# Two chunks of W side by side for each block of h in a LoRA feed-forward, with adapter passes grouped by block and PSUM waits by bank

## The chip, the cores and the metric

The kernel runs on one NeuronCore of one Trainium2 chip. The metric is the device time of one execution in microseconds (us); lower is better. TensorE, VectorE (DVE), ScalarE (ACT), GpSimd (POOL) and SyncE (SP) each follow their own list of instructions and meet at semaphores.

## The reference

Per batch of 8, with 512 rows (four tiles of 128) and 2048 columns:

```python
x = x + autocorrelation(layernorm(x), ctx, ctx)      # first block: spectra, top 12 lags, rolled sums
x = x + ffn(layernorm(x))                            # second block

def ffn(h):                                          # h: [8, 512, 2048], W: [2048, 2048]
    base = h @ W + bias
    A = einsum('bn,nri->bri', gate, lora_A)          # the batch's adapter, rank 32
    B = einsum('bn,nor->bor', gate, lora_B)
    return base + (h @ A.T) @ B.T + (h @ A_shared.T) @ B_shared.T
```

The change lies in the second block alone.

## The kernel before

Two blocks follow each other. The first computes the autocorrelation and stores `x2` in DRAM; it also splits W in two fp16 parts, `w_hi` and `w_lo`, and stores them. The second block loads all of W into SBUF (four chunks of 512 output columns, 16 blocks of 128 rows each) and runs over 32 tiles, `b` for the batch (0 to 7) and `t` for the tile in it (0 to 3), n = 4b + t. Batch 0 and batch 7 are written out, the others are a loop on some engines.

**h.** A tile of `x2` is loaded to one of two buffers `xt`. POOL adds the last row of `ctx` (`add_last`, L1292), DVE takes mean and variance (`statistics`, ends at `nb2`, L1472), ACT makes `h` (`normalise`, L1322) and its fp16 part, DVE the rest (`rest_of_h`, L1478), each in two halves, and ACT's queue issues four DMA transposes into `h_hi` and `h_lo` (L1334, L1336). POOL then adds the bias into `xt` (L1300). `h` of tile n+1 is made while TensorE works on tile n.

**TensorE.** A product in near fp32 is three fp16 passes: high by high, high by rest, rest by high. `chunk` (L1400) makes one bank of PSUM (0 to 3) from 16 blocks, 48 passes of 512 columns (L1412 to L1414). Each pass names its stationary block (here a block of `h`) and has a weight load of its own. In the middle of chunk 0 the small product `ax` is transposed (L1419). `adapter_out` (L1422) multiplies it with the adapters: for each of the four banks 4 to 7 one pass over 128 rows of `axT` (L1432) and one over 64 rows (L1433). `step` (L1435) is chunk 0, `adapter_out`, chunks 1, 2, 3, then `adapter_in` of the next tile (L1378), 48 passes of 64 columns that need all four transposes of the next `h`. `chunk` waits for `y_ok` to reach 4n: all four banks of the tile before have been read.

**DVE** (`step`, L1563) goes in a fixed order: rest of `ax`; `statistics` of the next tile; `finish` 0 (L1519: bank 0 into `xt`, waits for `y_spec` of that chunk, raises `y_ok`); `add_adapter` (banks 4 to 7, L1508); at t=3 the scales and the rest of the next batch's adapters; `finish` 1; `rest_of_h`; three sums of the next batch's adapter (`gated_sum`, L1532, each with a load `sg` from DRAM into one of two buffers; load i waits for sum i-2); `finish` 2; up to three more sums; at t=2 `largest` (L1541); `finish` 3; `adapter` of the next tile (`ax`, L1485). At t=2 only one sum stands between `finish` 2 and `largest`. Batch 7 has no sums.

**SP** goes in a fixed order too: the loads of `sg` for the tile; at t=2, once the last sum is done, the store of `b_next` (L1233) and, when that has landed, two loads of `b_f` (L1214); then it waits for `y_ok` 4n+4, stores `xt` to `out` (L1268), waits for that to land, loads `xt` for tile n+2 (L1210), and at t=2 the next `vl` (L1238).

```python
sp.wait_ge(y_ok, 4 * n + 4)
sp.dma_start(out_t[b, :, t, :], xt[:, t % 2, :]).then_inc(s_out[t % 2], 16)
...
finish(b, t, 2)
if gated and t < TT - 1:
    gated_part(b, t, 1)
...
finish(b, t, 3)
```

Of the kernel before, what the change touches and what calls it, by code (L numbers as in the profile page):

```python
# [41 lines left out]
KT = D // P  # L42
NL, RANK = 16, 32
# [38 lines left out]
def ahead(b, g, k):  # L82

    c = (g + k) // GPB
    return (b + c if c else b), (g + k) % GPB
# [7 lines left out]
def later(b, i):  # L93

    return not (isinstance(b, int) and b == 0 and i == 0)


def build(nc, x, ctx, gate, w, bias, lora_ab, lora_as, lora_bsT, fwd_tab, inv_tab, eye, nyq_mask, fwd_pair, out):
# [9 lines left out]
    with ExitStack() as outer:  # L108
        def sb(name, shape, dt=FP32, where=outer):
            return where.enter_context(nc.sbuf_tensor(name, shape, dt))  # L110

        def sem(name, where=outer):
            return where.enter_context(nc.semaphore(name))
# [19 lines left out]
        ps = outer.enter_context(nc.psum_tensor("ps", [P, 8, 512], FP32))  # L133
# [15 lines left out]
        s_w = [sem(f"s_w{k}") for k in range(8)]  # L149
# [1000 lines left out]
        with ExitStack() as st:  # L1150
            b_f = sb("b_f", [4 * RANK, D], FP32, st)
            b_hi = sb("b_hi", [4 * RANK, D], FP16, st)
            sb("early", [P, 79872 // 4], FP32, st)
            b_lo = early["b_lo"]
            h_hi = [early["h_hi0"], sb("h_hi1", [P, KT, P], FP16, st)]
            h_lo = [early["h_lo0"], sb("h_lo1", [P, KT, P], FP16, st)]
            w_hi, w_lo = [early["w_hi0"]], [early["w_lo0"]]
# [13 lines left out]
            axT = sb("axT", [4 * RANK, P], FP16, st)  # L1171
# [27 lines left out]
            d_spec = sem("d_spec", st)  # L1199
            d_ok = sem("d_ok", st)  # L1200
            y_spec = sem("y_spec", st)
            y_ok = sem("y_ok", st)

            with nc.Block() as block:
# [171 lines left out]
                @block.tensor  # L1376
                def _(pe):
                    def adapter_in(b, t):  # L1378

                        n, k = TT * b + t, t % 2  # L1380
                        pe.wait_ge(s_hh, 32 * n + 32)
                        for q in range(2):
                            pe.wait_ge(s_hl[q], 16 * n + 16)
                        if later(b, t):
                            pe.wait_ge(d_ok, 4 * n)
                        if t == 0:
                            pe.wait_ge(ab_lo, 16 * b + 8)
                        dst = ps[:, 4, 0:2 * RANK]
                        for i in range(KT):
                            high, rest = (a[:, i, :, :].rearrange("p s r -> p (s r)") for a in (a_hi, a_lo))  # L1390
                            nc.tensor.matmul(dst, h_hi[k][:, i, :], high, start=(i == 0), stop=False)  # L1391
                            nc.tensor.matmul(dst, h_hi[k][:, i, :], rest, start=False, stop=False)  # L1392
                            last = nc.tensor.matmul(dst, h_lo[k][:, i, :], high, start=False, stop=(i == KT - 1))  # L1393
                        last.then_inc(ax_spec, 1)

                    def bounds(b, bank, col):
                        pe.wait_ge(mx_ok, b + 1)
                        nc.tensor.matmul(ps[:, bank, col:col + 4], ones[:, :], mx[:, :], start=True, stop=True).then_inc(sc_spec, 1)

                    def chunk(b, t, c, gated):  # L1400
                        n, k = TT * b + t, t % 2
                        if c == 0:
                            pe.wait_ge(s_hh, 32 * n + 32)
                            for q in range(2):
                                pe.wait_ge(s_hl[q], 16 * n + 16)
                        if later(b, t):
                            pe.wait_ge(y_ok, 4 * n)
                        cols = slice(c * 512, (c + 1) * 512)
                        for i in range(KT):
                            if not later(b, t) and i % (KT // 2) == 0:  # L1410
                                pe.wait_ge(s_w[2 * c + i // (KT // 2)], 32)
                            nc.tensor.matmul(ps[:, c, :], h_hi[k][:, i, :], w_hi[c][:, i, :], start=(i == 0), stop=False)  # L1412
                            nc.tensor.matmul(ps[:, c, :], h_hi[k][:, i, :], w_lo[c][:, i, :], start=False, stop=False)  # L1413
                            last = nc.tensor.matmul(ps[:, c, :], h_lo[k][:, i, :], w_hi[c][:, i, :], start=False, stop=(i == KT - 1))  # L1414
                            if c == 0 and i == KT // 2:
                                pe.wait_ge(ax_ok, n + 1)
                                if gated and t == TT - 1:
                                    bounds(b + 1, 5, 2 * P)
                                nc.tensor.transpose(ps[:, 5, 0:P], ax[:, :, :].rearrange("p s r -> p (s r)"), ident[:, :]).then_inc(axt_spec, 1)  # L1419
                        last.then_inc(y_spec, 1)  # L1420

                    def adapter_out(b, t, gated):  # L1422

                        n = TT * b + t
                        pe.wait_ge(axt_lo, n + 1)
                        if gated and t == TT - 1:
                            pe.wait_ge(sc_read, b + 2)
                        if t == 0:
                            pe.wait_ge(ab_lo, 16 * b + 16)
                        for c in range(4):  # L1430
                            cols = slice(c * 512, (c + 1) * 512)
                            nc.tensor.matmul(ps[:, 4 + c, :], axT[:, :], b_hi[:, cols], start=True, stop=False)  # L1432
                            nc.tensor.matmul(ps[:, 4 + c, :], axT[0:2 * RANK, :], b_lo[0:2 * RANK, cols], start=False, stop=True).then_inc(d_spec, 1)  # L1433

                    def step(b, t, more, gated):  # L1435
                        chunk(b, t, 0, gated)
                        adapter_out(b, t, gated)
                        chunk(b, t, 1, gated)
                        chunk(b, t, 2, gated)
                        chunk(b, t, 3, gated)  # L1440
                        if more:
                            adapter_in(*ahead(b, t, 1))

                    bounds(0, 5, 2 * P)
                    adapter_in(0, 0)
                    for t in range(TT):
                        step(0, t, True, True)
                    for b in range(1, B - 1):
                        for t in range(TT):
                            step(b, t, True, True)  # L1450
                    for t in range(TT):
                        step(B - 1, t, t + 1 < TT, False)
# [190 lines left out]
```

## Time and profile before

| | |
|---|---|
| time, median of 3 runs | 3146.86 us (3145.36 to 3148.0) |
| the profiled execution | 3147.78 us, span 3146.0 us |
| TensorE busy | 3044.8 us (97%) |
| VectorE, ScalarE, GpSimd busy | 2080.5, 1117.0, 1675.4 us |
| mean granted TensorE clock | 0.988 |
| second block | about 1659 us to the end |
| passes of the four chunks (L1412 to L1414) | 3 x 2048, on the chain that ended last for 3 x 14% of the span |

A pass's busy time (379 ns) includes its way through the array and overlaps the next; how fast passes go is read from the distance between their starts. A clock of 1.00 is 2.4 GHz, 0.50 is 1.2 GHz. "idle before" names what ended the idle time of an engine.

### The profile page before, as it was taken

What the parts mean: (1) busy time and instruction counts of PE and PEld (TensorE: products, weight loads), DVE (VectorE), ACT (ScalarE), POOL (GpSimd) and SP (SyncE); (2) the same over time, 40 slices, a digit from 0 to 9 for tenths busy, and PEclk for the clock granted to TensorE, in tenths of its full rate; (3) what the DMA queues carried; (4) which work ended last, traced back from release to release, by engine and by line L of the source; (5) the groups of instructions that cost most, each with busy time, mean ns of one, the idle gap of its engine ahead of it and who ended that gap; (6) DMA issues with size and microseconds to landing.
All of it is one profiled execution on the core that took longest, in us unless ns stands there. A gap on an engine that the chain in (4) does not pass through costs nothing. (4 is left out here: it accounts for less than half of the span.)

```text
span 3146.0 us, 37959 instructions
## 1 busy us (share of the span) xinstructions
PE 3044.8 (97%) x14387; PEld 1642.7 (52%) x14387; DVE 2080.5 (66%) x2741; ACT 1117.0 (36%) x1696; POOL 1675.4 (53%) x753
## 2 busy tenths in 40 slices
PE   5999999999989999999977999999999999999999
PEld 3656566565656566566533444444444444444444
DVE  6899999999989999899984434443444444344321
ACT  4666666666656666555421110110111011011100
POOL 4888898888979898898651221221122112112210
PEclk8999999999999999999988999999999999999999
DMA  6334434344354534434259434344343534444321
GB/s 233 126 125 148 148 137 167 122 150 151 133 170 134 181 137 141 161 108 150 81 184 281 141 106 150 100 128 150 108 134 108 158 91 138 141 122 123 94 74 40
DMA packets 280787, 430.26 MB, mean 137 GB/s; under 512 B 147440, under 2 KB 163952, under 8 KB 265072
## 3 DMA queue, kind: packets, MB, share of 16 engines
q1 hardware_dynamic: 145456, 394.43, 36.0%
q10 hardware_dynamic: 135168, 33.57, 6.0%
q8 instruction: 113, 1.85, 0.2%
q14 instruction: 50, 0.41, 0.0%
HBM read 308.15 MB, written 86.25 MB: 125 GB/s over the span
## 5 line engine op out<-in xcount | busy, mean ns | idle before, releaser
L1412 PE MATMUL ps<-w_hi,h_hi 128*128 128x512 f16 x2048 | 776.8, 379 | 1.0 <-DVE xt L1519 1.0
L1413 PE MATMUL ps<-w_lo,h_hi 128*128 128x512 f16 x2048 | 776.4, 379 | 0.0
L1414 PE MATMUL ps<-w_hi,h_lo 128*128 128x512 f16 x2048 | 776.4, 379 | 0.0
L1292 POOL TENSOR_TENSOR xt<-xt,vl 128x2048 f32<-128x2048 f32 x31 | 139.6, 4503 | 919.4 <-DMA xt<-x_scratch 678.4
L877 PE MATMUL ps<-op,it 128*128 128x512 f32 x1024 | 447.3, 595 | 12.8 <-DVE op L1023 12.8
L802 PE MATMUL ps<-wt,fp 128*128 128x512 f16 x1536 | 338.3, 380 | 1.4 <-DVE wt L990 1.4
L1414 PEld LDWEIGHTS ps<-w_hi,h_lo 128*128 128x128 f16 x2048 | 200.4, 98 | 241.9 <-issue 0.4
L1412 PEld LDWEIGHTS ps<-w_hi,h_hi 128*128 128x128 f16 x2048 | 200.6, 98 | 240.9 <-issue 8.7
L877 PEld LDWEIGHTS ps<-op,it 128*128 128x128 f32 x1024 | 195.1, 191 | 247.3 <-issue 230.5
L1413 PEld LDWEIGHTS ps<-w_lo,h_hi 128*128 128x128 f16 x2048 | 200.5, 98 | 230.8 <-issue 0.3
L802 PEld LDWEIGHTS ps<-wt,fp 128*128 128x128 f16 x1536 | 150.5, 98 | 184.1 <-issue 1.9
L867 PE MATMUL ps<-it,cp 128*128 128x256 f32 x1024 | 230.7, 384 | 15.4 <-ACT cp L612 15.4
L1343 ACT ACTIVATE axT<-ps 128x128 f16<-128x128 f32 x32 | 8.9, 277 | 666.7 <-PE ps L1419 666.7
L1519 DVE SCALAR_TENSOR_TENSOR xt<-ps,w_back,xt 128x512 f32<-128x512 f32 x128 | 95.8, 748 | 209.0 <-PE ps L1414 198.6
L1461 DVE BATCH_NORM_STATS2 bn<-xt 128x6 f32<-128x512 f32 x124 | 76.6, 681 | 232.7 <-POOL xt L1292 232.7
L867 PEld LDWEIGHTS ps<-it,cp 128*128 128x128 f32 x1024 | 197.4, 193 | 46.7 <-ACT cp L612 16.4
L1532 DVE SCALAR_TENSOR_TENSOR ab<-sg,gt,ab 128x1024 f32<-128x1024 f32 x105 | 134.7, 1283 | 105.3 <-DMA sg<-lora_ab 104.4
L1322 ACT ACTIVATE h<-xt,nb,rs 128x2048 f32<-128x2048 f32 x31 | 64.9, 2095 | 371.5 <-DVE nb L1472 371.5
L1300 POOL TENSOR_TENSOR xt<-xt,brow 128x2048 f32<-128x2048 f32 x32 | 144.7, 4523 | 86.3 <-ACT h L1322 80.8
L452 POOL TENSOR_TENSOR cgl<-cg,uh 128x1024 fp32r<-128x1024 f32 x64 | 177.5, 2794 | 20.5 <-ACT uh L606 20.5
L475 POOL TENSOR_TENSOR cp<-eo 128x1024 f32<-128x1024 f32 x31 | 85.8, 2769 | 184.8 <-DVE cr L928 184.8
L794 PE MATMUL ps<-uh,fth 128*128 128x512 f32 x384 | 156.4, 407 | 17.2 <-POOL cgl L452 17.2
(190 smaller groups left out, 5724.2 us busy)
## 6 DMA issues: line engine op xcount, KB each, us to landing
sg<-lora_ab SPq DMA_DIRECT2D x112, 512.0 KB, 4.5
xv<-x SPq DMA_DIRECT2D x33, 1024.0 KB, 5.2
cg<-ctx SPq DMA_DIRECT2D x32, 1024.0 KB, 5.2
x_scratch<-xv SPq DMA_DIRECT2D x32, 1024.0 KB, 6.6
xt<-x_scratch SPq DMA_DIRECT2D x32, 1024.0 KB, 5.0
out<-xt SPq DMA_DIRECT2D x32, 1024.0 KB, 3.9
xg<-x SPq DMA_DIRECT2D x30, 1024.0 KB, 8.4
xrow<-x SPq DMA_DIRECT2D x24, 1024.0 KB, 6.0
```

The lines of the kernel that those rows point to most:

```text
L452: nc.gpsimd.tensor_tensor(cgl[:, k, 2 * h:2 * h + 2, :], cg[:, k, 2 * h:2 * h + 2, :], uh[:, 2 * h:2 * h + 2, :], ALU.subtract).then_inc(u ...
L794: last = nc.tensor.matmul(ps[:, TURN[kind], :], tab, val, start=(fresh and r == 0 and i == 0), stop=(r == 1 and i == 2), skip_group_check= ...
L802: last = nc.tensor.matmul(ps[:, bank, :], fp[:, tab, k, kind, :], pair[val][:, 2 * part + k, :], start=(k == 0 and i == 0), stop=(k == 1 a ...
L867: last = nc.tensor.matmul(ps[:, TURN[j], h * HALF:(h + 1) * HALF], cp[:, s, j * P:(j + 1) * P], it[:, s, :], start=(i == 0), stop=(i == 1))
L877: last = nc.tensor.matmul(ps[:, 4 + TURN[t], :], it[:, s, (t % 2) * P:(t % 2 + 1) * P], op[:, t // 2, s, :], start=(s == 0), stop=(s == 3))
L1292: nc.gpsimd.tensor_tensor(xt[:, k, :], xt[:, k, :], vl[:, :], ALU.add).then_inc(vl_ok, 1)
L1300: nc.gpsimd.tensor_tensor(xt[:, t % 2, :], xt[:, t % 2, :], brow[:, :], ALU.add).then_inc(bias_ok, 1)
L1412: nc.tensor.matmul(ps[:, c, :], h_hi[k][:, i, :], w_hi[c][:, i, :], start=(i == 0), stop=False)
L1413: nc.tensor.matmul(ps[:, c, :], h_hi[k][:, i, :], w_lo[c][:, i, :], start=False, stop=False)
L1414: last = nc.tensor.matmul(ps[:, c, :], h_lo[k][:, i, :], w_hi[c][:, i, :], start=False, stop=(i == KT - 1))
L1519: nc.vector.scalar_tensor_tensor(out=xt[:, k, cols], in0=ps[:, c, :], scalar=w_back[:, 0:1], in1=xt[:, k, cols], op0=ALU.mult, op1=ALU.add ...
L1532: nc.vector.scalar_tensor_tensor(out=ab[:, 0::2, :], in0=sg[:, i % 2, :, :], scalar=gt[:, i:i + 1], in1=ab[:, 0::2, :], op0=ALU.mult, op1= ...
```

## The change

Three edits, all in TensorE's list.

1. `chunk_pair` takes two chunks at once. For each block i it makes the four passes with `h_hi` (two chunks by `w_hi` and `w_lo`) and then the two with `h_lo`. The pair's last two passes raise `y_spec`, one after the other. The transpose of `ax` comes after block 8 of the first pair, `adapter_out` after the first pair.
2. `adapter_out` makes the four passes over 128 rows first and then the four over 64 rows.
3. The first pair waits for `y_ok` 4n-2 and the second for 4n.

DVE, SP, ACT and POOL keep their lists.

```diff
-                    def chunk(b, t, c, gated):
+                    def chunk_pair(b, t, first, gated):
                         n, k = TT * b + t, t % 2
-                        if c == 0:
+                        pair = (first, first + 1)
+                        if first == 0:
                             pe.wait_ge(s_hh, 32 * n + 32)
                             for q in range(2):
                                 pe.wait_ge(s_hl[q], 16 * n + 16)
                         if later(b, t):
-                            pe.wait_ge(y_ok, 4 * n)
-                        cols = slice(c * 512, (c + 1) * 512)
+                            pe.wait_ge(y_ok, 4 * n - 2 + first)
                         for i in range(KT):
                             if not later(b, t) and i % (KT // 2) == 0:
-                                pe.wait_ge(s_w[2 * c + i // (KT // 2)], 32)
-                            nc.tensor.matmul(ps[:, c, :], h_hi[k][:, i, :], w_hi[c][:, i, :], start=(i == 0), stop=False)
-                            nc.tensor.matmul(ps[:, c, :], h_hi[k][:, i, :], w_lo[c][:, i, :], start=False, stop=False)
-                            last = nc.tensor.matmul(ps[:, c, :], h_lo[k][:, i, :], w_hi[c][:, i, :], start=False, stop=(i == KT - 1))
-                            if c == 0 and i == KT // 2:
+                                for c in pair:
+                                    pe.wait_ge(s_w[2 * c + i // (KT // 2)], 32)
+                            for c in pair:
+                                nc.tensor.matmul(ps[:, c, :], h_hi[k][:, i, :], w_hi[c][:, i, :], start=(i == 0), stop=False)
+                                nc.tensor.matmul(ps[:, c, :], h_hi[k][:, i, :], w_lo[c][:, i, :], start=False, stop=False)
+                            for c in pair:
+                                last = nc.tensor.matmul(ps[:, c, :], h_lo[k][:, i, :], w_hi[c][:, i, :], start=False, stop=(i == KT - 1))
+                                if i == KT - 1:
+                                    last.then_inc(y_spec, 1)
+                            if first == 0 and i == KT // 2:
...
-                        last.then_inc(y_spec, 1)
...
                         for c in range(4):
-                            cols = slice(c * 512, (c + 1) * 512)
-                            nc.tensor.matmul(ps[:, 4 + c, :], axT[:, :], b_hi[:, cols], start=True, stop=False)
-                            nc.tensor.matmul(ps[:, 4 + c, :], axT[0:2 * RANK, :], b_lo[0:2 * RANK, cols], start=False, stop=True).then_inc(d_spec, 1)
+                            nc.tensor.matmul(ps[:, 4 + c, :], axT[:, :], b_hi[:, c * 512:(c + 1) * 512], start=True, stop=False)
+                        for c in range(4):
+                            nc.tensor.matmul(ps[:, 4 + c, :], axT[0:2 * RANK, :], b_lo[0:2 * RANK, c * 512:(c + 1) * 512],
+                                             start=False, stop=True).then_inc(d_spec, 1)
...
-                        chunk(b, t, 0, gated)
+                        chunk_pair(b, t, 0, gated)
                         adapter_out(b, t, gated)
-                        chunk(b, t, 1, gated)
-                        chunk(b, t, 2, gated)
-                        chunk(b, t, 3, gated)
+                        chunk_pair(b, t, 2, gated)
```

## Rows read from the trace of the kernel before

**Rows 1.** Windows: busy us and count by engine, granted clock, DMA share, GB/s.

```profile
2600.00:2800.00 200.00, 200.00 (x1079) 91.86 (x1077) 82.96 (x121) 24.31 (x21) 45.89 (x15) 1.00 0.42 126
```

**Rows 2.** Groups by form, passes and weight loads: busy us, mean ns | idle before.

```profile
L1412 PE MATMUL ps<-w_hi,h_hi 128*128 128x512 f16 x2048 | 776.8, 379 | 1.0 <-DVE xt L1519 1.0
...
L1413 PEld LDWEIGHTS ps<-w_lo,h_hi 128*128 128x128 f16 x2048 | 200.5, 98 | 230.8 <-issue 0.3
```

**Rows 3.** Timeline of PE, batch 1, t=2: `adapter_out`'s first pass, first passes of chunks 1 and 2.

```profile
1966.71 0.38 PE L1432 MATMUL ps<-b_hi,axT 128*128 128x512 f16 x1
...
1969.27 0.39 PE L1412 MATMUL ps<-w_hi,h_hi 128*128 128x512 f16 x1
...
1979.64 0.38 PE L1412 MATMUL ps<-w_hi,h_hi 128*128 128x512 f16 x1
```

**Rows 4.** Timeline of weight loads, end of an `adapter_out` and start of a chunk.

```profile
2013.35 0.09 PEld L1433 LDWEIGHTS ps<-b_lo,axT 64*128 64x128 f16 x1 [0.23 <-issue]
2013.67 0.10 PEld L1432 LDWEIGHTS ps<-b_hi,axT 128*128 128x128 f16 x1 [0.23 <-issue]
...
2014.97 0.10 PEld L1413 LDWEIGHTS ps<-w_lo,h_hi 128*128 128x128 f16 x1
```

**Rows 5.** Timeline of DVE, batch 5: `finish` 2 and 3 of t=2, `nb2` in t=3.

```profile
2722.20 0.75 DVE L1519 SCALAR_TENSOR_TENSOR xt<-ps,w_back,xt 128x512 f32<-128x512 f32 x1
...
2730.92 0.75 DVE L1519 SCALAR_TENSOR_TENSOR xt<-ps,w_back,xt 128x512 f32<-128x512 f32 x1 [5.49 <-PE ps L1414]
...
2751.74 0.21 DVE L1472 TENSOR_SCALAR nb<-mv,rs 128x1 f32<-128x1 f32 x1
```

**Rows 6.** Timeline of SP's queue, batch 5, t=2.

```profile
2724.20 0.33 SPq L1233 DMA_DIRECT2D b_next_scratch<-ab  x1
2726.27 0.80 SPq L1214 DMA_DIRECT2D b_f<-b_next_scratch  x2
2731.84 0.36 SPq L1268 DMA_DIRECT2D out<-xt  x1
```

**Rows 7.** Timeline of PE, batch 5: first pass of `adapter_in` behind t=2 and behind t=3.

```profile
2730.72 0.19 PE L1391 MATMUL ps<-a_hi,h_hi 128*128 128x64 f16 x1
...
2776.40 0.19 PE L1391 MATMUL ps<-a_hi,h_hi 128*128 128x64 f16 x1
```

**Rows 8.** Timeline of ACT's queue: last transposes issued in t=2 and t=3 of batch 5.

```profile
2715.78 1.36 ACTq L1336 DMA_TRANSPOSE h_lo<-h  x1
...
2770.45 1.36 ACTq L1336 DMA_TRANSPOSE h_lo<-h  x1
```

**Rows 9.** The line L1336: time from issue to landing of its transposes.

```profile
DMA to landing us min/median/max: 3.0/3.2/6.6
```

**Rows 10.** Timeline, batch 2, t=1: `nb2`, `finish` 2 and the store of `xt`.

```profile
2111.69 0.21 DVE L1472 TENSOR_SCALAR nb<-mv,rs 128x1 f32<-128x1 f32 x1
...
2130.16 0.74 DVE L1519 SCALAR_TENSOR_TENSOR xt<-ps,w_back,xt 128x512 f32<-128x512 f32 x1
...
2138.28 0.35 SPq L1268 DMA_DIRECT2D out<-xt  x1
```

**Rows 11.** Timeline of POOL, batch 5, t=3: `add_last`.

```profile
2743.39 4.50 POOL L1292 TENSOR_TENSOR xt<-xt,vl 128x2048 f32<-128x2048 f32 x1 [32.63 <-DMA vl<-ctx]
```

**Rows 12.** Timeline, batch 3: store of `xt` and next `add_last`, at t=1 and t=2.

```profile
2321.74 0.35 SPq L1268 DMA_DIRECT2D out<-xt  x1
...
2332.99 4.50 POOL L1292 TENSOR_TENSOR xt<-xt,vl 128x2048 f32<-128x2048 f32 x1 [31.11 <-DMA xt<-x_scratch]
...
2366.94 0.36 SPq L1268 DMA_DIRECT2D out<-xt  x1
...
2380.39 4.51 POOL L1292 TENSOR_TENSOR xt<-xt,vl 128x2048 f32<-128x2048 f32 x1 [32.06 <-DMA vl<-ctx]
```

**Rows 13.** Windows at the end of the first block, a long idle of PE and after.

```profile
1636.00:1641.00 5.00, 0.00 (x0) 0.00 (x0) 4.96 (x6) 0.00 (x0) 4.92 (x4) 0.50 0.66 214
1641.00:1643.00 2.00, 1.92 (x3) 0.89 (x4) 0.03 (x1) 0.03 (x1) 2.00 (x2) 0.50 0.47 184
```

## The prediction

> **What bounds the kernel now.** I read the windows first. In the second block (from 1659 us to the end) TensorE is busy without a gap at the full granted clock, 1.00, which is 2.4 GHz [rows 1]. The groups by form say the same: before the first passes of a block of `h` TensorE idled 1.0 us in the whole stage, and each of its weight loads has a record of its own, 98 ns against a pass that issues every 0.216 us [rows 2, 3]. So in this stage time is issued passes times their spacing, plus any new wait. Everything else (DVE's epilogue, the adapter sums, the chain that makes the next `h`) is hidden, and the question is how deep.
>
> Where passes are not 0.216 us apart, the timeline shows it. From one block of W to the next are 48 passes in 10.37 us, 0.216 each; the 8 passes of `adapter_out` take 2.56 us, 0.320 each [rows 3]. The loads tell why: between two passes over 128 rows the load starts with the pass ahead of it and costs nothing (L1413 at 2014.97, no idle), while between a 128-row pass and a 64-row one, either way, the load port idles 0.23 us first and the load then lies bare [rows 4].
>
> **Part 1, `adapter_out` by stationary block.** Before: high, low, high, low ..., eight changes of shape for a tile (the one into `chunk` 1 included). After: four high, four low, two changes. Six times 0.104 us is 0.62 us per tile, and 32 tiles give 20.0 us. The trace has no 64-row pass behind a 64-row pass. Bounds: if its load hides, like every load between passes of one shape, 20.0; if 64 rows themselves are the trouble, only the three high-after-high places gain, 0.31 per tile, 10.0 us. I take 20.0, since 128-row loads pay 0.104 as well when the shape changes.
>
> Beside this stands a rule of the Trainium skill ("TensorE: Matmul & The Clock Gate", Part 3, the mechanism): a load overlaps passes in flight only when its row group differs. By it no pass behind one of the same rows would gain, and this edit would be worth nothing. The trace disagrees for 128 rows, where 2048 loads of L1413 idle behind nothing [rows 2, 4]; for 64 rows no run here shows it, and my lower bound is that case.
>
> **Part 2, pairs of chunks.** No pass is dropped: 96 per pair, the same six per `i`. Four passes now share a stationary block, but each still issues its load: before, L1413 already repeats the block of L1412 and has 2048 loads [rows 2]. They were hidden, so this gives 0. Banks now alternate every two passes; `adapter_out` changes bank every two passes at no cost beyond the change of shape, so 0 too. The transpose moves from 5.8 to 11.7 us into a tile, and `ax` is there by then (below, +8).
>
> **Part 3, the waits by bank.** The first pair waits for two epilogues of the tile before instead of four: this takes away the 1.0 us [rows 2]. I count -1.0.
>
> **Part 4, what moves on DVE.** `y_spec` for chunk 2 no longer comes 10.4 us before chunk 3's, but one pass before it. DVE's order is fixed: `finish` 2, up to three adapter sums, `finish` 3. So in tiles 0 to 2 of a batch the second half of the sums, done under chunk 3 until now, stands between the end of the passes and `finish` 3. Behind `finish` 3 queue, on SP, the store of `xt` and the load of the tile after next; behind that load POOL's `add_last`, DVE's statistics, `normalise`, the transposes of `h`, and at last `adapter_in`, which waits for all four of them.
>
> The tightest place is the last tile of a batch (t=3), where ACT and DVE make the adapters too. I take batch 5. Let a be the start of `adapter_in` behind the passes of t=2 (2730.72). `finish` 3 starts at a+0.20, SP issues the store at a+1.12 [rows 5 to 7]. After the change `finish` 2 starts at a+0.20-0.22 = a-0.02. From its start to SP's `b_next` store are 2.00 us (finish and one sum), 2.07 until that has landed, 0.85 for the two loads of `b_f`: the store of `xt` is issued 4.92 later, at a+4.90, and `finish` 3, behind `largest`, is done by then [rows 5, 6]. The chain starts 3.78 us later. Before, it had this slack: last transpose issued 2770.45, landed 3.2 later at 2773.65, `adapter_in` at 2776.40, so 2.75 us [rows 7 to 9]. The deadline comes 0.62 earlier by part 1. Stall: 3.78 + 0.62 - 2.75 = **1.65 us**, in 7 batches (the last makes no adapters): 11.6 us.
>
> In t=0 and t=1, `finish` 2 to the store takes 8.1 us [rows 10] against 1.1: 7.0 later. The `h` made in the tile after each has more slack, read in t=2: a transpose issued at 2715.78 and landed at latest 6.6 on, against 2730.72, is 8.3 us, and 7.6 are needed [rows 7 to 9]. No stall in t=1 and t=2, but 0.7 us from one. `ax`, read behind `finish` 3, comes at about +8 in the next tile, before the transpose at 11.7.
>
> Not all batches are like 5. In batch 3, store to `add_last` is 13.45 us against 11.55 [rows 6, 11, 12]: +1.9. And in t=0 and 1 the loop closes on itself: `nb2` to the store 26.4, store to `add_last` 11.25, `add_last` to `nb2` 8.56 [rows 5, 10 to 12], 46.2 against a tile of 44.9, so DVE is late by itself and the store of t=2 is 2.3 later still. Batch 3: 1.65+1.9+2.3 = 5.9. The same working gives extras of 2.8, 1.3, 1.0 and 1.4 for batches 2, 1, 4 and 6, and -0.2 for batch 0. Extras together 10.5; stalls 22.1 us.
>
> Do such stalls cost clock? In an idle of the first block that fills a window of 5 us the clock was at 0.50 (1.2 GHz), and right behind it three passes filled 2 us [rows 13]. The stalls here are 1.5 to 4.6 in one piece; I count nothing, and 2 us a batch where it happens.
>
> **Small ends.** At the very end `finish` 2 and 3 follow each other: 0.75-0.22, +0.5. At the start, chunk 3 of W, the last to be loaded, is needed one chunk (10.4 us) earlier. It is needed in the first tile alone; I count 0 and keep 2 us for the range.
>
> **Sum.** -20.0 - 1.0 + 22.1 + 0.5 = +1.6 us on the profiled execution's 3147.78 (span 3146.0 and 1.8 around it), which lies 0.9 above the median: 3148.5, say **3149 us**. The gain in issue is given back in seven waits.
>
> **Rivals.** A change under 0.2% (6.3 us) can't be told from none here.
>
> *Faster: the chain fits.* One mechanism, the slack ahead of `adapter_in` in t=3. Each us less on the chain is 7 us. With batch 5's stall everywhere, 11.6 us in all: 3138. With none: 3146.9-20-1+0.5 = 3126.4. It decides once the mean stall is under 2.0 us instead of 3.2. For it: the long way from store to `add_last` (13.45 us, not 11.55) is that of the middle batches, and may not come back. Against: the slack is read at both ends, and SP's order is fixed. Chance 0.32.
>
> *Slower: 64-row loads stay bare.* Part 1 gives 10.0, the deadline is 0.31 kinder and the stalls fall by 2.2: +9.5, 3156. Against: the equal price of both directions [rows 4]. This is also what the skill's rule on row groups would leave. Chance 0.12.
>
> *Slower: the chain is later than computed.* Sums waiting longer for loads of `sg` that now collide with the store and the transposes, t=2 stalling too, or the clock falling in the long stalls: 1 to 2 us a batch, 3156 to 3163. For it: t=0 and t=1 have 0.7 us left. Chance 0.17.
>
> *Bank changes cost clock.* A rule of the Trainium skill (same page, "A second HAM failure mode") has passes that cycle through PSUM banks let the clock swing between its levels. Here, `adapter_out` cycles through four banks and the clock is 1.00 over 200 us [rows 1, 3]. If a tenth of the 6144 passes ran at half clock it would be +133 us, 3280. Chance 0.02.
>
> *The pairing doesn't save loads* is in the forecast. If loads were dropped after all, the time is the same, since they are hidden.
>
> **Numbers.** Forecast 0.37 (3141 to 3154 as its own range), faster 0.32, bare loads 0.12, late chain 0.17, clock 0.02. Faster by over 0.2%: 0.31; within: 0.38; slower: 0.31. The range goes from half of the faster case's stalls to the late chain: 3131 to 3163.
>
> **What would show it.** `adapter_out` in 1.94 us with six passes 0.216 apart (right) or 2.25 (bare). As many loads as passes. `finish` 3 of t=0 and 1 some 8 us behind the passes. The first `adapter_in` pass of t=3 waiting for a transpose of `h_lo`, seven times, 1.5 to 4.6 us, none in the last batch. Wrong would be: waits in t=1 or t=2 as well, a store of `xt` at t=2 earlier than 3.8 us behind its old place, or a clock under 1.00 there.

## The result, and the profile after

The changed kernel takes 3168.4 us (median of 4; 3166.0 to 3171.6) against 3147.4 for the one before: ratio 1.0066, 95% interval [1.0054, 1.0078], 21 us slower. The forecast was 3149 with a range up to 3163. What it named as the cost is there, in its place and seven times, but about twice as dear.

First what was to be gained. The timeline of the changed kernel around an `adapter_out` (start, duration; "x4" is four passes in a row):

```profile
2674.34 0.74 PEld L1435 LDWEIGHTS ps<-b_hi,axT 128*128 128x128 f16 x4
2674.56 1.03 PE L1435 MATMUL ps<-b_hi,axT 128*128 128x512 f16 x4
2675.51 0.54 PEld L1437 LDWEIGHTS ps<-b_lo,axT 64*128 64x128 f16 x4 [0.42 <-issue]
2675.52 1.03 PE L1437 MATMUL ps<-b_lo,axT 64*128 64x512 f16 x4
2676.48 0.10 PEld L1414 LDWEIGHTS ps<-w_hi,h_hi 128*128 128x128 f16 x1 [0.42 <-issue]
2676.48 0.39 PE L1414 MATMUL ps<-w_hi,h_hi 128*128 128x512 f16 x1
```

The eight passes take 1.92 us instead of 2.56 [rows 3]. Only the two loads at a change of shape come late (the 0.42 us of idle); those between 64-row passes are hidden like the others. 0.64 us a tile, 20 us in all, as forecast. A tile without a wait is now 44.88 us from start to start, and 45.51 before.

The waits of the second block (us in total, times, longest us) and the groups, passes only (busy us, mean ns | idle before):

```profile
PE ps L1391 <- issue: 28.3, 7, 4.8
```

```profile
L1414 PE MATMUL ps<-w_hi,h_hi 128*128 128x512 f16 x2048 | 780.2, 381 | 0.0
...
L1391 PE MATMUL ps<-a_hi,h_hi 128*128 128x64 f16 x512 | 56.6, 204 | 32.2 <-issue 28.3 <-DVE a_lo L1499 3.9
L1437 PE MATMUL ps<-b_lo,axT 64*128 64x512 f16 x128 | 33.1, 379 | 0.0
...
L1435 PE MATMUL ps<-b_hi,axT 128*128 128x512 f16 x128 | 32.9, 379 | 0.0
```

The 1.0 us in front of the first pass of a block is gone [rows 2]. In its place stand seven waits ahead of `adapter_in`, 28.3 us by the view (it counts from the modelled end of the last pass, 0.17 us later than the next pass could start). "issue" names no releaser; the chain of batch 5, from t=2 into t=3, shows what it is. The same rows of before are [rows 5 to 9, 11]:

```profile
2742.08 0.75 DVE L1522 SCALAR_TENSOR_TENSOR xt<-ps,w_back,xt 128x512 f32<-128x512 f32 x1 [1.48 <-PE ps L1417]
2742.10 0.19 PE L1391 MATMUL ps<-a_hi,h_hi 128*128 128x64 f16 x1
...
2742.75 1.28 DVE L1535 SCALAR_TENSOR_TENSOR ab<-sg,gt,ab 128x1024 f32<-128x1024 f32 x1
2744.05 0.33 SPq L1233 DMA_DIRECT2D b_next_scratch<-ab  x1
2744.06 1.22 DVE L1544 TENSOR_REDUCE mx<-ab 128x2 f32<-128x1024 f32 x1
2745.20 0.74 DVE L1522 SCALAR_TENSOR_TENSOR xt<-ps,w_back,xt 128x512 f32<-128x512 f32 x1
...
2746.12 0.80 SPq L1214 DMA_DIRECT2D b_f<-b_next_scratch  x2
2747.21 0.36 SPq L1268 DMA_DIRECT2D out<-xt  x1
2752.79 0.37 SPq L1210 DMA_DIRECT2D xt<-x_scratch  x1
...
2761.14 4.51 POOL L1292 TENSOR_TENSOR xt<-xt,vl 128x2048 f32<-128x2048 f32 x1 [31.73 <-DMA vl<-ctx]
...
2769.50 0.21 DVE L1475 TENSOR_SCALAR nb<-mv,rs 128x1 f32<-128x1 f32 x1
...
2788.21 1.36 ACTq L1336 DMA_TRANSPOSE h_lo<-h  x1
...
2791.64 0.21 PE L1391 MATMUL ps<-a_hi,h_hi 128*128 128x64 f16 x1 [4.32 <-issue]
```

With a = 2742.10: `finish` 2 starts at a-0.02, the store of `b_next` is issued at a+1.95, the loads of `b_f` at a+4.02, the store of `xt` at a+5.11 (before: a+1.12). Then `add_last` 13.93 us later (before 11.55), `nb2` 8.36, the last transpose 18.71, `adapter_in` 3.43. The steps to `nb2` and to the last transpose are those of before, and the transpose lands after 3.2 us as before; the first pass follows 0.2 us later. TensorE was ready at a+45.05 and starts at a+49.54: 4.5 us late. The distances from last pass to `adapter_in`, less one pass, are 3.9, 3.7, 3.9, 4.0, 4.9, 4.5 and 4.6 us in batches 0 to 6: 29.5 us.

And this is not all. Windows from TensorE's last pass of that tile on (the last columns are the granted clock, the DMA share and GB/s):

```profile
2787.00:2791.00 4.00, 0.32 (x2) 0.00 (x0) 2.47 (x3) 0.00 (x0) 0.00 (x0) 0.98 0.78 166
2791.00:2796.00 5.00, 4.36 (x53) 3.29 (x54) 0.29 (x1) 0.00 (x0) 0.00 (x0) 0.50 0.59 216
2796.00:2798.00 2.00, 2.00 (x7) 0.71 (x6) 0.00 (x0) 0.00 (x0) 0.00 (x0) 0.58 0.98 410
2798.00:2800.00 2.00, 2.00 (x11) 0.89 (x10) 0.00 (x0) 0.00 (x0) 0.88 (x1) 1.00 0.53 129
```

TensorE idles from 2787 to 2791.6. The clock is still at full level for nearly all of the first window, at 0.50 (1.2 GHz) in the second, and back at 1.00 only in the last. `adapter_in` takes 2.53 us instead of 1.40, and the tile behind it begins slowly. The seven tiles t=3 are 49.7 to 51.1 us long against 45.05, 37.1 us too much in sum, and the seven behind them 45.04 to 46.61 against 44.88, 6.1 too much. Of these 43.2 us, 29.5 are waiting and 13.7 the clock.

The balance of the profiled executions over the 31 tiles from start to start: 43.2 - 19.5 (regrouping) - 1.4 (the waits at chunk 0 and what followed them) = +22.3, which is the difference of 1436.6 us (after) and 1414.3 (before). The medians are 21 us apart.

### The profile page after: what moved, and what is told of

The parts are those of the page before. It is cut to its first block and busy times, and to the rows that moved or that the text cites. A ratio compares the mean times of both kernels' runs of the same rounds, so it can differ in the third digit from the quotient of the medians.

```text
span 3165.6 us, 37962 instructions
## 1 busy us (share of the span) xinstructions
PE 3039.0 (96%) x14387; PEld 1649.8 (52%) x14387; DVE 2097.7 (66%) x2741; ACT 1117.5 (35%) x1696; POOL 1676.9 (53%) x753
## 5 line engine op out<-in xcount | busy, mean ns | idle before, releaser
L1417 PE MATMUL ps<-w_hi,h_lo 128*128 128x512 f16 x2048 | 610.4, 380 | 0.0
L877 PE MATMUL ps<-op,it 128*128 128x512 f32 x1024 | 447.4, 595 | 12.8 <-DVE op L1023 12.8
L867 PEld LDWEIGHTS ps<-it,cp 128*128 128x128 f32 x1024 | 197.8, 193 | 44.9 <-ACT cp L612 14.4
L1494 DVE TENSOR_TENSOR axT<-ps,axT 64x128 f16<-64x128 f32 x32 | 9.4, 295 | 286.9 <-ACT axT L1343 286.9
```

The source lines that it names most:

```text
L867: last = nc.tensor.matmul(ps[:, TURN[j], h * HALF:(h + 1) * HALF], cp[:, s, j * P:(j + 1) * P], it[:, s, :], start=(i == 0), stop=(i == 1))
L877: last = nc.tensor.matmul(ps[:, 4 + TURN[t], :], it[:, s, (t % 2) * P:(t % 2 + 1) * P], op[:, t // 2, s, :], start=(s == 0), stop=(s == 3))
```

## The experiments

The kernel before was timed beside each group of runs: 3148.0 us in both. Ratios are to it.

**The regrouping alone.** The kernel before with edit 2:

```diff
                         for c in range(4):
-                            nc.tensor.matmul(ps[:, 4 + c, :], axT[:, :], b_hi[:, cols], start=True, stop=False)
-                            nc.tensor.matmul(ps[:, 4 + c, :], axT[0:2 * RANK, :], b_lo[0:2 * RANK, cols], start=False, stop=True).then_inc(d_spec, 1)
+                            nc.tensor.matmul(ps[:, 4 + c, :], axT[:, :], b_hi[:, c * 512:(c + 1) * 512], start=True, stop=False)
+                        for c in range(4):
+                            nc.tensor.matmul(ps[:, 4 + c, :], axT[0:2 * RANK, :], b_lo[0:2 * RANK, c * 512:(c + 1) * 512],
+                                             start=False, stop=True).then_inc(d_spec, 1)
```

> The kernel before with the second edit alone (adapter_out: four passes over 128 rows, then four over 64). Theory A (two changes of shape instead of eight, 0.104 us each, and nothing becomes late since DVE's order meets the same chunks): 8 passes in 1.94 us, 20 us less, 3127 us, no wait of the first adapter_in pass. Rival B (64-row loads stay bare): the low passes 0.32 us apart, 10 us less, 3137. Rival C (the rule that a load hides only behind another row group): no gain, 3147.

3132.4 us, ratio 0.9949 [0.9933, 0.9966]: 16 us faster. Tiles are 44.88 us, rivals B and C are out. The missing 4 us are in its waits:

```profile
PE ps L1412 <- DVE xt L1520: 6.8, 6, 2.3
```

This is the view of the profiled execution, which is 3 us slower than the median; it would account for more than the 4 us. "Nothing becomes late" was wrong. A tile that is 0.63 us shorter meets a DVE that is as slow as ever, and chunk 0, which waits for all four banks, waits for `finish` 3 of the tile before, six times and 6.8 us instead of 1.0. TensorE's waits of up to 2.3 us here left the clock at 1.00.

**The pairs without the regrouping.** The changed kernel with edit 2 undone.

> The changed kernel with the second edit undone: pairs and waits by bank, adapter_out as before (high, low, high, low). Theory A (the edits add up: the regrouping is worth 0.62 us in each of 32 tiles, the waits of t=3 come 0.62 us later on TensorE's side and shrink by as much): 14 to 16 us slower than the changed kernel, about 3183, waits of adapter_in 3.3 to 4.5 us, the same lower clock behind them. Rival B (bank changes every two passes are what slows the pair): passes inside a pair more than 0.216 us apart.

3179.7 us, ratio 1.0104 [1.0089, 1.0120]. A tile without a wait is 45.51 us, as before the change: neither pairing nor changing the bank every two passes costs or gains on TensorE itself. The waits:

```profile
PE ps L1391 <- issue: 23.6, 7, 4.2
```

Seven again. By the distances 24.8 us are waiting and 9.9 the clock, 34.7 in sum. The regrouping is worth 12 us on top of the pairs (1.0104 to 1.0066), not 20: 8.5 of the 20 go into longer waits (4.7) and more time at the low clock (3.8). The expectation had the first and took the second as unchanged.

**The sums ahead of finish 2.** In the changed kernel, on DVE:

```diff
                         if gated and t < TT - 1:
                             gated_part(b, t, 0)
-                        finish(b, t, 2)
-                        if gated and t < TT - 1:
                             gated_part(b, t, 1)
                             if t == TT - 2:
                                 dve.wait_ge(g_ok, NL * b + NL)
                                 largest(b + 1)
+                        finish(b, t, 2)
                         finish(b, t, 3)
```

> The changed kernel with both halves of the adapter sums and largest ahead of finish 2 on DVE, so that finish 2 and finish 3 follow the pair at once. Theory A (the waits come from the sums between finish 2 and finish 3, through the store of xt): finish 3 about 1.4 us behind the passes, the store at t=2 some 3 us earlier, waits of adapter_in in t=3 under 1 us or none, no lower clock there, 3127 to 3131 us. Rival B (the pairing itself, by its banks or its later chunks, is what costs): the waits and most of the 21 us stay, over 3155.

3130.8 us, ratio 0.9945 [0.9928, 0.9961]: 38 us less than the changed kernel, and nothing of the pairing was touched. Rival B is out. One wait above 1 us is left, in the batch where the last sum was late and the store of `xt` stood behind the loads of `b_f` (its SP queue, then TensorE's waits):

```profile
2715.13 0.33 SPq L1233 DMA_DIRECT2D b_next_scratch<-ab  x1
2717.19 0.80 SPq L1214 DMA_DIRECT2D b_f<-b_next_scratch  x2
2718.27 0.36 SPq L1268 DMA_DIRECT2D out<-xt  x1
```

```profile
PE ps L1391 <- issue: 2.7, 1, 2.7
```

**The wait filled with work.** In the changed kernel, on TensorE, passes that nobody reads (`adapter_in` starts bank 4 anew):

```diff
                         chunk_pair(b, t, 2, gated)
+                        if gated and t == TT - 1:
+                            pe.wait_ge(d_ok, 4 * (TT * b + t) + 4)
+                            for i in range(17):
+                                nc.tensor.matmul(ps[:, 4, :], h_hi[t % 2][:, i % KT, :], w_hi[3][:, i % KT, :], start=True, stop=True)
                         if more:
```

> The changed kernel with 17 more passes of 512 columns (3.7 us at full clock) into bank 4 behind the last pair of each t=3 tile of batches 0 to 6, whose results are overwritten by adapter_in. They fill most of TensorE's wait of 3.9 to 5.1 us. Theory A (behind each wait the clock is at its lower level for some microseconds, 12 us in all): the waits shrink to 0.2 to 1.5 us, the clock stays 1.00, the kernel is 10 to 12 us faster than the changed one, about 3157, although it does more work. Rival B (the time behind the waits has another cause, such as late work of DVE): same time as the changed kernel, 3168, or slower where the filling overshoots.

3153.3 us, ratio 1.0017 [1.0007, 1.0026]: with 119 more passes it is 15 us faster than the changed kernel. Windows of batch 5, t=3, and its passes:

```profile
2777.00:2781.00 4.00, 4.00 (x21) 1.78 (x19) 1.57 (x3) 1.06 (x1) 0.00 (x0) 1.00 0.42 79
2781.00:2784.40 3.40, 3.40 (x17) 1.55 (x16) 1.16 (x2) 0.00 (x0) 0.00 (x0) 1.00 1.10 285
2784.40:2788.00 3.60, 3.60 (x60) 2.38 (x59) 0.29 (x1) 0.00 (x0) 0.00 (x0) 1.00 0.47 175
```

```profile
2780.77 3.83 PE L1447 MATMUL ps<-w_hi,h_hi 128*128 128x512 f16 x17
2784.44 0.19 PE L1391 MATMUL ps<-a_hi,h_hi 128*128 128x64 f16 x1
```

All seven tiles t=3 are 48.7 us (45.05 + 3.68), those behind them 44.88: no time at the low clock. By the distances that saves the 13.7 us, and 3.7 more since the waits beyond 3.68 us are gone too; by the medians both together are 15. The chain itself is shorter here: store to `add_last` takes 12.8 to 13.1 us, against 12.7 to 14.4 in the changed kernel. The DMA rows show what goes with it. The profile has a queue of kind "instruction", with packets of 16 KB. In the changed kernel such a packet falls between the store and 12 us behind it in batches 4, 5 and 6 (13.9 to 14.4 us) and not in batches 1 to 3 (12.7 to 13.1) nor in batch 0, which takes 13.6 all the same; here it does in no batch. No run moved such a packet on purpose, so that it is the cause isn't shown.

**The store of xt first.** In the changed kernel, on SP, `load_next_b` being the five lines taken out:

```diff
-                        if t == TT - 2:
-                            sp.wait_ge(g_ok, NL * b + NL)
-                            sp.wait_ge(ab_lo, 16 * b + 16)
-                            sp.dma_start(b_next, ab[:, 2, :]).then_inc(s_bst, 16)
-                            sp.wait_ge(s_bst, 16 * b + 16)
-                            load_b(b + 1, b_next)
...
                                 load_last(b + 1)
+                        if gated and t == TT - 2:
+                            load_next_b(b)
```

> The changed kernel with SP's list turned round at t=2: the store of xt, the loads of xt and vl first, then the store of b_next and the loads of b_f. Theory A (my price missed that the store now shares the DMA engines with the loads of b_f, 5.6 us instead of 4.0 until the next load, vl 0.8 us slower, and stands behind them for 1.1 us): the chain is 3.5 us shorter per batch, waits of adapter_in 0.4 to 1.6 us, mostly too short for the clock to fall, 3131 us (3127 to 3137). Rival B (the stores are slow by themselves, as in the middle batches before): only 1.1 us per batch, 3160; or the adapters come late and high_of_ab waits for b_f, which would eat the gain.

3145.9 us, ratio 0.9998 [0.9988, 1.0007]: 21 us less than the changed kernel, not 37. Batch 5 again:

```profile
2729.83 0.35 SPq L1268 DMA_DIRECT2D out<-xt  x1
2733.86 0.34 SPq L1210 DMA_DIRECT2D xt<-x_scratch  x1
2734.47 0.34 SPq L1238 DMA_DIRECT2D vl<-ctx  x1
2734.99 0.33 SPq L1233 DMA_DIRECT2D b_next_scratch<-ab  x1
...
2742.43 4.51 POOL L1294 TENSOR_TENSOR xt<-xt,vl 128x2048 f32<-128x2048 f32 x1 [28.67 <-DMA vl<-ctx]
```

The store until SP's next load is back at 4.03 us (5.58 with the loads of `b_f` beside it), and at 3.9 to 4.0 in six of the seven batches (one 5.86; the changed kernel has 5.3 to 6.6 in all seven), so sharing was the cause of that part, against rival B. The one of 5.86, like the slow stores of batches 1 to 3 in the kernel before, has a packet of the instruction queue beside it. The DMA rows of the kernel before, from the issue of the store to the next load, in batch 2 (5.38 us) and in batch 5 (4.03 us), give packets, MB and share of the 16 engines by queue:

```profile
q1 hardware_dynamic: 144, 1.05, 47.3%
q8 instruction: 1, 0.02, 1.4%
...
q1 hardware_dynamic: 144, 1.05, 62.2%
```

In the nine traces together 246 stores have no loads of `b_f` in the 2 us ahead of them. 104 of these have such a packet beside them, and 142 have none. The 142 take at most 4.5 us; of the 104, 49 are no slower than 4.6 us and 55 are, up to 6.3. Where loads of `b_f` go just ahead and no such packet is near, 19 stores take 5.3 to 5.7 us.

`vl` still takes 7.96 us until `add_last`, and `finish` 2 was itself 0.4 us late behind a sum. The waits are 1.1 to 3.2 us, 14.9 in sum. The five of up to 2.5 us left the clock at 1.00; behind the two of over 3 us, in batches 4 and 6, it was lower, which cost 4.3 us. The wait of batch 5 and what follows, then batch 6:

```profile
2770.40:2772.90 2.50, 0.12 (x1) 0.02 (x1) 1.36 (x2) 0.00 (x0) 0.00 (x0) 1.00 0.80 172
2772.90:2777.90 5.00, 4.99 (x65) 3.07 (x66) 0.29 (x1) 0.00 (x0) 0.00 (x0) 1.00 0.63 220
2952.60:2955.80 3.20, 0.22 (x3) 0.07 (x3) 1.41 (x2) 0.00 (x0) 0.00 (x0) 0.97 1.01 226
2955.80:2960.80 5.00, 5.00 (x59) 3.56 (x59) 0.29 (x1) 0.00 (x0) 0.00 (x0) 0.68 0.65 220
```

The expectation was right in kind, but forecast a gain of 37 us where 21 came.

**Two ways out.** The kernel before with edit 2 and, in the old order of four chunks, a wait by bank:

```diff
                         if later(b, t):
-                            pe.wait_ge(y_ok, 4 * n)
+                            pe.wait_ge(y_ok, 4 * n - 3 + c)
```

> The kernel before with the regrouped adapter_out and, in the old order of four single chunks, a wait for the one bank that the chunk writes (y_ok 4n-3+c instead of 4n for all). Theory A (a shorter tile makes chunk 0 wait for finish 3 of the tile before, 6.8 us in all with the regrouping alone): no wait at L1412, 6 to 7 us less than the regrouping alone, 3125 us. Rival B (the wait moves to the next place that is late, adapter_in's four transposes or ax): 3129 to 3132 as with the regrouping alone.

And the changed kernel with both lists mended, DVE's and SP's, as in the two diffs above.

> The changed kernel with both lists mended: all adapter sums ahead of finish 2 on DVE, and on SP the store of xt ahead of the store of b_next and the loads of b_f. Theory A (what is left with the sums first is one wait of 2.7 us in the one batch whose store stands behind late loads of b_f): no wait of adapter_in, 2 to 4 us less than with the sums first alone, 3127 us, and the same as the regrouping with waits by bank, since pairing by itself is worth nothing. Rival B (pairing is worth something once nothing waits): below 3120.

The first takes 3126.1 us, ratio 0.9932 [0.9918, 0.9945]; the second 3129.8, 0.9944 [0.9931, 0.9958]. In the first TensorE doesn't stand still once the tiles have begun (a thousand microseconds in one window):

```profile
1700.00:2700.00 1000.00, 999.95 (x5542) 466.78 (x5541) 445.76 (x595) 114.38 (x99) 218.08 (x68) 1.00 0.44 132
```

It has the lowest median, 22 us below the kernel before and 42 below the changed one, and it has no pairs. Rival B of either run is out: the first has no new wait in its trace, and no run of the second is below 3126. By the medians the second isn't faster than the sums first alone (0.9945): the wait of 2.7 us that it was to remove is small beside these intervals. In the traces it is gone (two waits of 0.8 us in sum are left), and from the first tile to the last it is 3.5 us shorter, 1394.8 us against 1398.3. The first kernel has 1393.8 there, and the two intervals overlap, so nothing shows a difference between pairs and single chunks. Both gains of the change, the regrouping and the waits by bank, are had without pairs.

## Why the prediction was wrong, by its own steps

**Right.** The price of `adapter_out` (0.62 us a tile forecast, 0.64 seen). Pairing worth nothing, since the loads were hidden and are all still issued. No cost of bank changes: clock and spacing of the passes as before. Also the place of the new wait, its number (7), batch 7 without one, the chain through DVE, SP and POOL, and that tiles t=0 to t=2 stay free of it.

**The step that failed** is the price of the stalls, 22.1 us against 43.2.

- *"I count nothing" for the clock*: 13.7 us, the larger part. The forecast took an idle at the low clock from the first block [rows 13] and left out that a wait of 4 us could end there too. It had the size right in the rivals ("2 us a batch where it happens"; it was 2.0) and the case wrong. Its own sign of being wrong, "a clock under 1.00 there", came. The Trainium skill ("TensorE: Matmul & The Clock Gate", HAM oscillation) warns of just this, waits long enough to throttle a loop again and again; the windows above agree.
- *The waits themselves*: 29.5 against 22.1. For batch 5, 2.4 of the 2.8 us missing are in "store to `add_last` 11.55", which was read where the store ran by itself. The change moved it next to the loads of `b_f`; measured it is 13.93, and 12.7 to 14.4 over the batches. The rest is the store issued 0.2 later than counted and 0.2 us from the landing to the first pass, which weren't counted. The extras for the middle batches were read as belonging to the batch; this no longer held: in the kernel before, the store was slow in batches 1 to 3 alone (5.3 to 6.0 us, 3.9 to 4.1 in the others), in the changed one it is slow in all seven, and the longest waits are in batches 4, 5 and 6, those with a packet of the instruction queue beside the chain. Part of the sum came out by luck: batch 3 was forecast at 5.9 us and is 4.0, batch 5 at 1.65 and is 4.5. The loop that was to close on itself didn't close. In t=1 and t=2 of every batch with sums `finish` 2 starts right behind the passes, so DVE isn't late by itself, and the store of t=2 in batch 3 is 0.6 us later than in batch 5, not 2.3.

The two misses add up to 21.1 us, and the time is 19 above the forecast. The rival "the chain is later than computed" was the right one, with 0.17 where it needed more, and its two parts (DMA and clock) came together, not one or the other; that took the time 5 us beyond the range.

## What to carry to other kernels

Making two chunks ready at once takes nothing from TensorE, but gives everything that DVE did between them one deadline: count what stands between the last pass and the store that frees the next buffer. A chain that moves takes its DMAs into new company; price them by a place where they share, not where they ran alone. And a wait of some 4 us on TensorE is priced with the slow microseconds behind it, here 2.0 us for each. Changes of the row count of the stationary block are worth grouping wherever they alternate.

## What the runs showed of the hardware

- A weight load hides behind a pass over the same rows, 64 or 128, and not where the number of rows changes, in either direction: 0.104 us each.
- In seven waits of 3.7 to 4.9 us between long runs of passes the clock fell to 0.50, between 2.2 us before work came back and 0.5 us after, and the first microseconds of work ran at half speed. Useless passes in the same place kept it at 1.00 and made the kernel 15 us faster. Waits of 1.1 to 2.5 us, in the run with the store first, cost no clock.
- A 1 MB store with two small loads issued about 1 us ahead of it took 5.3 to 6.6 us until SP's next load, in all seven batches of the changed kernel. With the store put first it was 3.9 to 4.0 in six of seven.
- A 16 KB packet of the instruction queue goes with slow transfers: all 55 stores of over 4.6 us that had no such loads just ahead have one beside them, and the 142 stores with neither take 4.5 us at most. Whether it is the cause wasn't tested.
